# Attention and a top-4 expert layer on one Trainium2 core: 160 expert tiles of 128 rows against 112 tiles of 128 rows and 32 tiles of two 64-row pieces

## What is computed

```python
scores = softmax(xf @ Wg)                      # 4096 tokens, 32 experts
weights, indices = top_k(scores, 4)            # 16384 (token, expert) pairs
for e in range(32):
    tok = the tokens that chose e              # at most 2048 of them
    out = (silu(xf[tok] @ W1[e]) * (xf[tok] @ W3[e])) @ W2[e] * w[:, None]
    y = y.at[tok].add(out)
z = (silu(xf @ Ws1) * (xf @ Ws3)) @ Ws2        # shared expert, every token
out = x + y + z
```

## Time and profile before

| | us |
|---|---|
| median of 3 runs (lowest, highest) | 621.23 (620.42, 621.5) |
| time of the profiled execution | 622.96 |
| its span | 621.2 |
| TensorE busy | 581.0 (94% of the span) |
| ScalarE busy | 411.3 (66%) |
| POOL busy | 374.3 (60%) |
| VectorE busy | 350.8 (56%) |
| mean granted TensorE clock | 0.986 of full |

### The profile page before, as it was taken

The page is one execution under the profiler, slowest core; times in us unless marked ns, Lnnn a source line. Parts: engine busy times, 40 slices in busy tenths (PEclk is TensorE's granted clock), DMA queues, the critical chain, the costliest instruction groups (busy, mean ns, idle before and its releaser), DMA issues.

```text
span 621.2 us, 16830 instructions
## 1 busy us (share of the span) xinstructions
PE 581.0 (94%) x4081; PEld 420.3 (68%) x4081; DVE 350.8 (56%) x1420; ACT 411.3 (66%) x1338; POOL 374.3 (60%) x425
## 2 busy tenths in 40 slices
PE   4799999999999988699989999999999999999988
PEld 1366766667666765257767888888888888854555
DVE  4589999999999996632222232323232322316773
ACT  2589989889898984304656667676767666644541
POOL 4114777877878777622544555655565655549970
PEclk9999999999999998689999999999999999999999
DMA  8995444444444545966776555555555655539993
GB/s 277 306 275 176 184 179 156 174 187 175 165 165 175 188 176 185 346 228 206 243 224 211 175 190 183 183 183 183 187 179 182 185 189 175 190 114 411 409 376 111
DMA packets 70155, 130.54 MB, mean 210 GB/s; under 512 B 10288, under 2 KB 48560, under 8 KB 70064
## 3 DMA queue, kind: packets, MB, share of 16 engines
q1 hardware_dynamic: 52128, 83.32, 41.2%
q0 software_dynamic: 13824, 41.96, 18.3%
q10 hardware_dynamic: 4112, 4.19, 2.0%
HBM read 61.11 MB, written 68.32 MB: 208 GB/s over the span
## 4 chain that ended last, share of the span: by engine, by line
PE 70%; POOL 10%; issue 7%; DVE 6%; ACT 3%; SPq 3%; DMA 1%; POOLq 0%; ACTq 0%; DVEq 0%
PE pS L792 21%; PE pS L804 10%; PE pS L615 9%; POOL xs L380 6%; PE pQV L721 4%; PE pS L652 3%; PE pT L785 3%; PE pO L738 3%; PE pQV L785 3%; POOL w L398 2%; PE pQV L630 2%; PE pO L630 2%; PE pO L704 1%; PE pT L693 1%; PE pO L799 1%
## 5 line engine op out<-in xcount | busy, mean ns | idle before, releaser
L409 POOL DMA_INDIRECT ys<-gsh,dst x160 | 153.7, 960 | 131.1 <-ACT gsh L545 129.3
L792 PE MATMUL pS<-w,after_a 128*128 x640 | 166.3, 382 | 0.2 <-ACT after_a L534 0.2
L380 POOL DMA_INDIRECT xs<-xg,posi x128 | 124.5, 972 | 49.5 <-issue 25.9
L792 PEld LDWEIGHTS pS<-w,after_a 128*128 128x128 f32 x640 | 109.1, 190 | 10.3 <-issue 0.5
L804 PE MATMUL pS<-w,after_a 128*128 x320 | 95.7, 381 | 0.0
L1076 DVE COPY after_a<-pT 128x128 f32<-128x128 f32 x80 | 23.4, 292 | 94.1 <-PE pT L799 94.1
L545 ACT ACTIVATE gsh<-pS,xg 128x256 f32<-128x256 f32 x160 | 75.9, 474 | 0.4 <-issue 0.4
L1076 DVE COPY after_a<-pO 128x128 f32<-128x128 f32 x80 | 23.3, 292 | 93.2 <-PE pO L799 92.1
L544 ACT CAST dst<-xg 128x1 int32 x160 | 30.6, 191 | 60.3 <-PE pS L804 59.5
L721 PE MATMUL pQV<-w 128*128 128x512 f32 x128 | 64.0, 624 | 0.5 <-ACT w L475 0.5
L615 PE MATMUL pS<-x2T_all,ws 128*128 128x512 f32 x128 | 61.2, 633 | 2.3 <-DVE gsh L1039 1.4
(11 more groups left out here) (158 smaller groups left out, 1081.1 us busy)
## 6 DMA issues: line engine op xcount, KB each, us to landing
xg<-xs SPq DMA_DIRECT2D x160, 160.0 KB, 2.2
ys<-gsh SPq DMA_DIRECT2D x32, 512.0 KB
w<-ys SPq DMA_DIRECT2D x32, 512.0 KB, 15.5
xs<-padrow SPq DMA_DIRECT2D x33, 160.0 KB, 2.3
w<-in_L_ffn_W ACTq DMA_DIRECT2D x1, 4096.0 KB, 21.9
out<-xall SPq DMA_DIRECT2D x32, 128.0 KB, 2.6
xall<-in_L_attn_X SPq DMA_DIRECT2D x1, 3072.0 KB, 13.8
ys<-gsh,dst POOLq DMA_INDIRECT x160, 2.7
```

What stands on the lines that cost most here:

```text
L380: pool.indirect_dma_start(out=xs, out_offset=bass.IndirectOffsetOnAxis(ap=posi[:, a.r8, k:k + 1], axis=0), in_=xr[:, a.r8, :], in_offset=N ...
L409: pool.indirect_dma_start(out=ys, out_offset=bass.IndirectOffsetOnAxis(ap=dst[:, j % 8:j % 8 + 1], axis=0), in_=y[:, j % 8, :], in_offset= ...
L792: last = pe.matmul(pS[a.b][:, 0:2 * F], xgT[:, a.b, k, :], w13[:, bass.ds(e, 1), k, :, :].rearrange("p a n f -> p (a n f)"), start=(k == 0 ...
```

## The change

NU = 16384/128 - 16 = 112 tiles still have 128 rows of one expert. NH = 32 tiles have two pieces of 64 rows, each of any expert. That is 144 tiles. Tiles 0 to 47 are whole; from tile 48 on every third (50, 53, ... 143) has halves. The whole tiles of all experts are counted out first in even numbers of 64-row pieces, and what is left of each expert goes to the pieces. The table now has 65 ranges in place of 32.

In a tile of halves each product becomes one for each half: 64 columns of the array, all 128 rows, output on partitions 0 to 63 or 64 to 127. The first half reads its weights in place by register; the second half's weights are copied by VectorE to a fixed place in `x2T_all` (which is free at that time), two buffers deep. ScalarE copies destinations and scales in two instructions each. SP loads such a tile with two DMAs of 64 rows. A pad is 64 rows, is stored behind the first two of every three loads below 48, and only tiles of halves wait for pads (for all 32 of them).

```diff
-    NJ = PAIRS // P + E
+    HB = P // 2
+    NH = E
+    NU = PAIRS // P - E // 2
+    NJ = NU + NH
+    FIRST_HALF = NJ - 3 * NH
+    NE = 2 * E + 1
...
+    def in_halves(j):
+        return j >= FIRST_HALF and j % 3 == 2
...
+        def w13_second(j, k):
+            return x2T_all[:, half_number(j) % 2, k * 2 * F:(k + 1) * 2 * F]
...
-        DVE_CONSTS = 17
+        DVE_CONSTS = 23
...
-                sp.dma_start(xs[bass.ds(at, P)], padrow[:]).then_inc(padded[e % 8], 16)
-
-            for e in range(AHEAD):
-                store_pad(e)
+                sp.dma_start(xs[bass.ds(at, HB)], padrow[0:HB, :]).then_inc(S["padded"], 16)
+
...
                 wait(sp, S["y_done"], j - 7)
-                if j < E:
-                    sp.wait_ge(padded[j % 8], 16 * (j // 8 + 1))
-                sp.dma_start(xg[:, j % 8, :], xs[bass.ds(at, P)]).then_inc(loaded[j % 8], 16)
-                if j + AHEAD < E:
-                    store_pad(j + AHEAD)
+                if in_halves(j):
+                    sp.wait_ge(S["padded"], 16 * E)
+                    for h in range(2):
+                        r = block_at[(2 * j + h) % 4]
...
+                        sp.dma_start(xg[h * HB:(h + 1) * HB, j % 8, :], xs[bass.ds(at, HB)]).then_inc(loaded[j % 8], 16)
+                else:
...
+                    sp.dma_start(xg[:, j % 8, :], xs[bass.ds(at, P)]).then_inc(loaded[j % 8], 16)
+                if j < FIRST_HALF and j % 3 < 2:
+                    store_pad(2 * (j // 3) + j % 3)
...
+                    if in_halves(a.t):
+                        e = [expert_of(a, h) for h in range(2)]
+                        for h in range(2):
+                            act.copy(dst[h * HB:(h + 1) * HB, a.r8:a.r8 + 1], xg[h * HB:(h + 1) * HB, a.r8, bass.ds(e[h] + DST, 1)])
+                        act.activation(y[0:HB, a.r8, :], pS[2 + a.b][0:HB, 0:D], ACT.Copy, scale=xg[0:HB, a.r8, bass.ds(e[0] + D, 1)])
+                        act.activation(y[HB:P, a.r8, :], pS[2 + a.b][HB:P, 0:D], ACT.Copy, scale=xg[HB:P, a.r8, bass.ds(e[1] + D, 1)]
+                                       ).then_inc(S["y_done"], 1)
...
+                    if in_halves(a.t):
+                        e = expert_of(a)
+                        pe.wait_ge(S["w13_staged"], half_number(a.t) + 1)
+                        for k in range(KC):
+                            for h in range(2):
+                                last = pe.matmul(pS[a.b][h * HB:(h + 1) * HB, 0:2 * F], xgT[:, a.b, k, h * HB:(h + 1) * HB],
+                                                 w13_second(a.t, k) if h else w13_of(e, k), start=(k == 0), stop=(k == KC - 1))
...
+                        pe.wait_ge(S["w2_staged"], half_number(a.t) + 1)
+                        for h in range(2):
+                            last = pe.matmul(pS[2 + a.b][h * HB:(h + 1) * HB, 0:D], geT[:, a.b, h * HB:(h + 1) * HB],
+                                             w2_second(a.t) if h else w2_of(e), start=True, stop=True)
...
+                if (a := tile_of(-1)) is not None and in_halves(a.t):
+                    wait(dve, S["y_ps"], a.t - 5)
+                    dve.tensor_copy(x2T_all[:, half_number(a.t) % 2, 0:KC * 2 * F],
+                                    w13[:, bass.ds(second_of(a.t), 1), :, :, :].rearrange("p a k n f -> p (a k n f)")
+                                    ).then_inc(S["w13_staged"], 1)
+                if (a := tile_of(0)) is not None and in_halves(a.t):
+                    wait(dve, S["y_ps"], a.t - 5)
+                    dve.tensor_copy(w2_second(a.t), w2[:, bass.ds(second_of(a.t), 1), :].rearrange("p a c -> p (a c)")
+                                    ).then_inc(S["w2_staged"], 1)
```

More of the change, by code:

```diff
@@ L247, in build @@
         NPRE = 2
-        AHEAD = 4
         QT = TG // P
@@ L525, in _, with expert_of @@
                 shared_silu(g)
-            number = [act.alloc_register(f"act_expert{n}") for n in range(4)]
+            number = [[act.alloc_register(f"act_expert{h}_{n}") for n in range(4)] for h in range(2)]
             act.wait_ge(S["erow_done"], 1)
+            def expert_of(a, h=0):
+                r = number[h][a.r4]
+                act.reg_load(r, erow[0:1, column(a.t, h):column(a.t, h) + 1])
+                return nc.s_assert_within(act.snap(r), 0, E - 1, skip_runtime_bounds_check_because="the table holds experts 0 .. E-1 only")
             def expert_step(tile_of):
@@ L1069, in _, with second_of @@
             shared_add(NPRE - 1)
+            second_at = [dve.alloc_register(f"second{n}") for n in range(2)]
+            def second_of(j):
+                r = second_at[half_number(j) % 2]
+                dve.reg_load(r, erow[0:1, column(j, 1):column(j, 1) + 1])
+                return nc.s_assert_within(dve.snap(r), 0, E - 1, skip_runtime_bounds_check_because="the table holds experts 0 .. E-1 only")
+            dve.wait_ge(S["h_ps"], FC * NPRE)
+            dve.wait_ge(S["w13_in"], 16 * 2 * KC)
+            dve.wait_ge(S["w2_in"], 16)
             def expert_step(tile_of):
```

115 lines of the change are left out of this document (78 added, 37 removed).

## The result

The changed kernel takes **639.75 us** (median of 4 runs, 638.98 to 642.56), the kernel before 621.1 (620.42 to 621.5): ratio 1.030, 95% interval 1.026 to 1.034. It is 18.6 us slower where I forecast 8 us faster. The span of the profiled execution goes from 621.2 to 637.2 us.

A forecast was written before the change was run, and what follows sets the result against it. TensorE was taken as the bound, with SP's DMAs slowing the first tiles. Terms -26.0 - 7.0 + 21.1 + 1.3 + 2.1 + 0.5 = -8.0 gave 613.2 us against the median, range 605 to 620.5.

The forecast's parts named there:

- ScalarE, I put it at 0: ScalarE's added work in tiles of halves: given back in the two whole passes behind, cost 0.
- rival C: ScalarE becomes the bound in tiles of halves: +9.6 us, giving 622.8 us; chance 0.06.
- The sign that I had set: From tile 48 on, three tiles take about 5.54 us; differing by more than 0.3 us means the forecast is wrong.
- Sixteen tiles, -26.0: TensorE's expert tiles: 144 in place of 160, at 1.627 us each, save 26.0 us.
- Blocks, +21.1 (15.4 to 26.9): TensorE going into and out of half-product blocks: 0.33 us each, two per tile of halves, +21.1 us.
- Rival A: Half products on TensorE don't run side by side: +41.3 us, giving 654.5 us; chance 0.10.
- D: Rival: a block of half products costs TensorE next to nothing, giving 592 us; chance 0.07, with half-way prices.
- SP's queue, -7.0: SP's loads and pads before tile 48: fewer DMAs remove the whole loss there, -7.0 us, at worst -3.5.
- Rival B: SP stays the bound of the first tiles, the 7.0 us stay, giving 620.2 us; chance 0.12.
- Constants and table, +1.3 and +2.1: Before tile 0: six more constant instructions cost 1.3 us, eight more table instructions 2.1 us.
- VectorE, 0: VectorE's two weight copies for each tile of halves fit in its free time, cost 0.
- The end, +0.5: The last tile has halves; its longer way over ScalarE delays the last scatter, +0.5 us (0 to 1.2).

The follow-up runs named there:

- e14: Changed kernel with ScalarE's register loads moved ahead of the silu, right behind the copy of the rows: 617.5 us, ratio 0.993 to the kernel before.
- e11: Changed kernel with ScalarE's register loads moved ahead of its two waits, on a faster chip: 622.1 us, ratio 1.000 to the kernel before.
- e2: Changed kernel with one ScalarE eviction of 128 rows in place of two of 64 in tiles of halves: 669.5 us, ratio 0.992 to the kernel before.
- e17: Same edit as e2 on the changed kernel (one eviction of 128 rows), run again: 670.6 us, ratio 0.990 to the kernel before.
- e12: Changed kernel with VectorE gathering scale and destination columns for tiles of halves, on a faster chip: 615.4 us, ratio 0.990 to the kernel before.
- e15: Changed kernel with columns gathered by VectorE and whole tiles' register load ahead of the silu, on a slower chip: 655.8 us, ratio 0.970 to the kernel before.
- e4: Changed kernel with register loads ahead of the waits and whole products in tiles of halves: 680.7 us, ratio 1.011 to the kernel before.
- e5: Same edit as e11 on the changed kernel (loads ahead of the waits), on a slower chip: 683.4 us, ratio 1.024 to the kernel before.
- e6: Same edit as e12 on the changed kernel (columns gathered by VectorE), on a slower chip: 668.6 us, ratio 1.000 to the kernel before.

## Why the prediction was wrong

**The step that failed is "ScalarE, I put it at 0".** It named the mechanism, as rival C: ScalarE late with its copy in tiles of halves, TensorE waiting for it, at 622.8 us and with a chance of 0.06. The sign that I had set was there: three tiles take 6.17 us where I wanted 5.54 within 0.3. What the step had wrong is its size, in two ways.

- *What is added.* I counted 0.6 us (a CAST at 0.12 and an ACTIVATE) and named a register load without a price. Measured, the way goes from 0.61 to 2.20 us, +1.59. Piece by piece, by the timeline above against the earlier trace rows: product's end to first column copy 0.82 us, before 0.12 (+0.70, the loads); first copy to first eviction 0.40, before 0.12 (+0.28, the second copy and its register arithmetic); a second eviction (+0.49); from there to the copy of the rows 0.49, before 0.37 (+0.12). I read the diff as the same load, doubled, and did not see that `expert_of` had gone from ahead of the two waits to behind them. Well ahead it costs nothing (`e14`), behind it is on the way; `e14` and `e11` differ from the changed kernel in that alone, and by 23 and 18 us on chips on which the kernel before takes 621.9. Nor do the loads make the wait alone: with them left where they are, one eviction less brings the third pass to 1.70 (`e2`, `e17`).
- *What is free.* I argued that the copy is needed only a pass later and that two whole passes give it back, and gave no number. The table has it: 0.91 us are free over the 0.61 of a whole tile, thanks to the longer second pass. With my own 0.6 the step would have been 0, rightly. With the true 1.59 it is 0.68 a tile of halves in thirty tiles, and **+21.3 us** from tile 48 to the last by the difference to `e12`. Rival C's 0.3 was 0.6 less the idle time of 0.35 in a pass; that idle time is not the free part of the way.

**The rest stood.**

- *Sixteen tiles, -26.0*: whole passes are 1.63 before and after.
- *Blocks, +21.1 (15.4 to 26.9)*: (1.98 - 1.63) + (1.87 - 1.63) = 0.59 us a tile of halves, 18.9 us, of which `e12` shows 18.3 up to the last tile; the whole-product runs bring all passes back to 1.63. I had one price for both blocks; the one with two pairs costs 0.24, the one with four 0.35. Rival A falls (pairs start 0.01 us apart) and so does D. Of what the Trainium skill, "TensorE: Matmul & The Clock Gate", "Measured speedup vs the span model", gives a packed group, one matmul's duration and about 4 ns for each further tile, the trace agrees with the pairs: the second starts 6 to 7 ns after the first, which the page's 4 ns is a little under. From the first pair to the second it takes 0.267 us, from there on 0.216 (medians of the changed kernel's trace). The 0.24 and 0.35 for a block come on top of the products' own time.
- *SP's queue, -7.0*: -6.2 in the trace, 4.8 of it brought back by the old order of pads. Rival B falls.
- *Constants and table, +1.3 and +2.1*: TensorE's first transposes of the weights go from 20.72 to 21.67, the wait for the table from 1.45 to 3.71 us, tile 0 starts 4.1 us later (286.49; I said 285.8). These two waits make 3.2 of it. The other 0.9 goes with the clock, which I had put at 0: behind the longer wait the granted clock is 0.50 for 6.8 us (266.3 to 273.1), before for 3.4.

```profile
21.67 0.69 PE L762 MATMUL pT<-ident,w 128*128 128x128 f32 x2 [5.62 <-DVE w L1009]
```

```profile
265.96 0.72 PE L806 MATMUL pT<-ident,ejc 128*1 128x128 f32 x4 [3.71 <-DVE ejc L1113]
```

```profile
268.60:272.00 3.40, 3.04 (x4) 1.49 (x5) 0.91 (x2) 0.00 (x0) 1.85 (x2) 0.50 0.74 286
```

- *VectorE, 0*: right, and still right with four more instructions in each tile of halves.
- *The end, +0.5*: +4.6. Same root and one more. TensorE's next work waits for the last eviction, after it the clock falls:

```profile
564.02 0.38 PE L868 MATMUL pS<-x2T_all,after_a 128*64 128x256 f32 x1
566.75 6.63 PE L664 MATMUL pS<-x2T_all,ws 128*128 128x512 f32 x11 [2.35 <-ACT gsh L589]
```

```profile
566.70:570.10 3.40, 3.35 (x4) 1.51 (x5) 0.00 (x0) 0.00 (x0) 0.96 (x1) 0.50 0.22 77
```

  The shared expert's products (L664) start 8.70 us after the last tile's transposes, before 5.74; that is 3.0 of the 4.6. Then 3.4 us pass at a granted clock of 0.50, the 1.2 GHz level, which is work of 1.7 us at 2.4 GHz.

Put together, the measured sizes give the difference of the spans: 4.1 - 6.2 - 26.0 + 18.3 + 21.3 + 4.6 = +16.1, against 637.2 - 621.2 = 16.0. With ScalarE's step at 0 and the end at 0.5 as I had them it is -9.3. `e12`, where ScalarE is relieved, has a span of 612.9 us, 8.3 under the 621.2 of the kernel before, and its median is 6.5 under the one measured beside it. So apart from the failed step and what hangs on it at the end, my -8.0 fits that kernel within 2 us, in part because errors cancel: the blocks cost 2.8 less than I said, the start 1.6 more and the first tiles 1.0 more.

What stays open: why the ratio of `e15` is 0.970 on a chip of the slower kind (three executions) when its parents give 0.990 and 0.993 on a faster one.

## What to carry to other kernels

When an engine gets more work between two waits, don't ask how busy it is: take from the trace the way from the releasing event to the instruction that somebody waits for, and the free time of that way, and put the added work against it. Look in the diff for register loads that changed sides of a wait; the profile doesn't count them as busy and blames their time on the engine that was waited for. And measure a cost (here the blocks) only in a kernel in which no other wait can take up what is saved, as ScalarE's way did in `e4`.

## What the runs showed of the hardware

- *A semaphore that comes 1.0 us late.* In both runs of the kernel with the loads first on slower chips, ScalarE's wait for the second half product ended 0.98 and 0.95 us after the product's recorded end in the median (0.05 in the changed kernel on both kinds of chip, in 30 tiles each); VectorE, waiting for the same semaphore, went on within 0.01 us of it. In one case of `e5` the semaphore of the half product (recorded end 541.436) and that of the following transposes (541.804) arrived at 542.482 and 542.525, 43 ns apart, while the one of the next products (542.819) came 24 ns after its end: by the records, whose ends of products are modelled, TensorE's own work is not late, only the news of it. With whole products and the loads first (`e4`) it was 1.06. These three kernels have the loads ahead of the waits and ran on slower chips. Without loads ahead of the waits the median behind the half product was 0.05 there too (`e2`, `e6`, `e15`, `e17`), with single ones 1 us late or more; but in `e6` the median behind the product of the tile after it was 0.39. On the chip of the fourth batch ScalarE went on 0.05 us after the end in `e14` and 0.16 in the median of `e11`. Whether the loads' place makes the semaphore late on slower chips is not settled: `e14`, whose loads are through earlier, did not run on one. What holds the semaphore up is open; it was enough to turn a gain of 18 us into a loss of 5.
- *Half clock after a pause.* Behind the last tile TensorE stood idle 0.66 us (`e12`) and 0.80 (before) and went on at full clock. After 1.97 us (`e14`) and 2.36 (the changed kernel in the third batch) the rows show 0.50 for 6.8 us, after 2.35 in the first trace and 1.73 in `e2` and `e17` for 3.4, and in `e11`, after a pause of 1.97 us as well, no fall:

```profile
544.08 1.12 PE L662 MATMUL pS<-x2T_all,ws 128*128 128x512 f32 x2 [0.66 <-ACT gsh L587]
```

```profile
544.10:550.90 6.80, 6.80 (x16) 3.12 (x17) 0.69 (x1) 0.60 (x1) 1.72 (x2) 1.00 0.47 155
```

```profile
543.53 2.08 PE L664 MATMUL pS<-x2T_all,ws 128*128 128x512 f32 x2 [1.97 <-ACT gsh L590]
```

```profile
542.50:549.30 6.80, 5.77 (x7) 2.52 (x8) 0.00 (x0) 0.95 (x3) 1.55 (x2) 0.50 0.37 134
```

  The first two are `e12`, the last two `e14`. From the last tile to the end they take 75.0 and 79.3 us, and that is why `e14` is the slower of the two: from tile 0 to the last it is 0.7 us ahead.
- *Small ScalarE operations overlap.* A column copy of 0.19 us adds 0.09 to the way when its register is ready, and 0.20 when register arithmetic stands ahead of it.
